# Row maximum of two of sixteen attention steps taken in two passes, one for each PSUM bank of scores

## What is computed

```
att = jnp.einsum('bqhd,bkhd->bhqk', q, k) * scale
att = jnp.where(causal, att, -jnp.inf)
att = jax.nn.softmax(att, axis=-1)
y = jnp.einsum('bhqk,bkhd->bqhd', att, v)
```

## Time and profile before

| | us |
|---|---|
| median of 3 runs | 3212.84 (3212.77 to 3213.65) |
| the profiled execution's own time | 3214.32 |
| its span | 3212.5 |
| PE busy | 3121.6 (97% of the span) |
| DVE busy | 2058.3 (64%) |
| ACT busy | 1946.8 (61%) |
| POOL busy | 1547.1 (48%) |
| granted TensorE clock | 0.993 of full |

### The profile page before, as it was taken

The page is one execution under the profiler, slowest core; times in us unless marked ns, Lnnn a source line. Parts: engine busy times, 40 slices in busy tenths (PEclk is TensorE's granted clock), DMA queues, the critical chain, the costliest instruction groups (busy, mean ns, idle before and its releaser), DMA issues. The chain is left out here.

```text
span 3212.5 us, 62152 instructions
## 1 busy us (share of the span) xinstructions
PE 3121.6 (97%) x20524; PEld 2515.9 (78%) x20524; DVE 2058.3 (64%) x5922; ACT 1946.8 (61%) x4189; POOL 1547.1 (48%) x1623
## 2 busy tenths in 40 slices
PE   8999999999999999999999999989989999999996
PEld 6777776777777677777777777769989999999996
DVE  5676666666667666666666666663878874445445
ACT  6676676666667666676766667655544444444444
POOL 3343343434434343343434434336766776666655
PEclk9999999999999999999999999999989999999998
DMA  5444454444445444444444444447744444433425
GB/s 135 103 116 97 102 126 102 107 115 94 109 102 125 102 105 112 97 112 115 108 103 106 109 115 112 99 139 267 282 156 96 105 118 103 106 88 88 107 49 155
DMA packets 213234, 376.61 MB, mean 117 GB/s; under 512 B 26280, under 2 KB 136232, under 8 KB 212928
## 3 DMA queue, kind: packets, MB, share of 16 engines
q1 hardware_dynamic: 170880, 322.20, 38.5%
q0 software_dynamic: 25152, 33.75, 6.2%
q10 hardware_dynamic: 16896, 16.78, 1.5%
HBM read 129.28 MB, written 75.59 MB: 64 GB/s over the span
## 5 line engine op out<-in xcount | busy, mean ns | idle before, releaser
L232 POOL TENSOR_SCALAR prob<-prob,inv 128x128 f32<-128x128 f32 (+7 forms) x1024 | 775.6, 757 | 1283.5 <-DVE inv L665 1276.7
L660 DVE CUSTOM_DVE_ANT_0 s_ps<-s_ps,mask 128x128 f32<-128x128 f32 (+7 forms) x1024 | 781.5, 763 | 659.9 <-PE s_ps L373 643.6
L550 ACT ACTIVATE prob<-s_ps,neg_max 128x128 f32<-128x128 f32 (+7 forms) x1024 | 759.6, 742 | 340.9 <-DVE neg_max L660 325.7
L388 PE MATMUL t_ps<-ident,prob 128*128 128x128 f32 x4096 | 611.3, 274 | 1.0 <-ACT prob_t L643 0.5
L643 ACT ACTIVATE prob_t<-t_ps 128x512 f32<-128x512 f32 (+3 forms) x704 | 376.8, 535 | 280.7 <-PE t_ps L388 274.0
L404 PE MATMUL o_ps<-prob_t,v 128*64 128x512 f32 (+3 forms) x3072 | 537.5, 492 | 1.5 <-DVE c_res L683 1.5
L388 PEld LDWEIGHTS t_ps<-ident,prob 128*128 128x128 f32 x4096 | 474.8, 140 | 52.6 <-issue 2.8
L404 PEld LDWEIGHTS o_ps<-prob_t,v 128*64 128x64 f32 x3072 | 204.1, 136 | 286.1 <-issue 267.2
L732 DVE COPY prob_t<-t_ps 128x128 f32<-128x128 f32 (+3 forms) x704 | 321.4, 456 | 27.6 <-PE t_ps L388 27.5
L1678 PE MATMUL e_y<-w_hi,hid_hi 128*128 128x256 f32 (+1 forms) x1088 | 312.2, 287 | 0.0
L1680 PE MATMUL e_y<-w_hi,hid_lo 128*128 128x256 f32 (+1 forms) x1088 | 308.2, 283 | 0.0
(11 more groups left out here) (259 smaller groups left out, 6226.0 us busy)
## 6 DMA issues: line engine op xcount, KB each, us to landing
k_hh<-k_high SPq DMA_DIRECT2D x128, 256.0 KB, 4.2
y_d<-c_res SPq DMA_DIRECT2D x128, 256.0 KB, 3.9
k_lz<-k_low SPq DMA_DIRECT2D x126, 256.0 KB, 5.1
w_lo<-k_high SPq DMA_DIRECT2D x124, 256.0 KB, 4.1
c_yt<-y_d SPq DMA_DIRECT2D x60, 512.0 KB, 6.9
q_hl<-q_high SPq DMA_DIRECT2D x64, 256.0 KB, 3.5
q_hl<-q_low SPq DMA_DIRECT2D x64, 256.0 KB, 4.3
b_xt<-w SPq DMA_DIRECT2D x16, 1024.0 KB
```

The source lines that it names most:

```text
L232: pool.tensor_scalar(pr, pr, inv[:, s % 4:s % 4 + 1], 1.0, ALU.mult, ALU.mult).then_inc(norm_done, 1)
L388: mm = pe.transpose(turned_in(s, k)[:, j * P:(j + 1) * P], prob[s % 4][:, (first + j) * P:(first + j + 1) * P], ident[:])
L550: act.activation(prob[s % 4][:, 0:(q + 1) * P], s_ps[s % 2][:, 0:(q + 1) * P], ACT.Exp, scale=-1.0, bias=neg_max[:, s % 4:s % 4 + 1], accu ...
L660: dve.tensor_tensor_reduce(part, part, mask[:, T - (q + 1) * P:T], 1.0, -MASKED, ALU.add, ALU.min, neg_max[:, s % 4:s % 4 + 1]).then_inc(m ...
```

## The change

In steps 13 and 15 of each pair TensorE signals `scores_done` after each of the two banks, 18 signals a pair where there were 16. VectorE's `maximum` runs two instructions there: a `tensor_reduce` with the minimum over the first bank's 512 columns, which the mask does not touch, into `neg_first`, and then the old instruction over the second bank's columns alone (384 in step 13, 512 in step 15), with `neg_first` as its beginning. Before the second there is a wait for the first one's own signal on `max_done`, a wait for the second bank, and a `sem_inc`. `max_done` too has 18 signals a pair. `scored(n, s)` gives the count at which step s is whole, and `exp` and the one wait of SyncE go by it. Nothing else moves.

```diff
+        neg_first = sb("neg_first", [P, 1])
...
+        BY_BANK = (13, 15)
+
+        def scored(n, s):
+
+            n, s = n + s // 16, s % 16
+            return (16 + len(BY_BANK)) * n + s + 1 + sum(t <= s for t in BY_BANK)
...
-                    sp.wait_ge(scores_done, 16 * (NPAIRS - 1))
+                    sp.wait_ge(scores_done, scored(NPAIRS - 2, 15))
...
-                mm.then_inc(scores_done, 1)
+                    if c == g or s in BY_BANK:
+                        mm.then_inc(scores_done, 1)
...
-                act.wait_ge(max_done, 16 * n + s + 1)
+                act.wait_ge(max_done, scored(n, s))
...
-                dve.wait_ge(scores_done, 16 * n + s + 1)
+                least, width, first = neg_max[:, s % 4:s % 4 + 1], (q + 1) * P, -MASKED
+                begin = 0
+                if s % 16 in BY_BANK:
+
+                    dve.wait_ge(scores_done, scored(n, s) - 1)
+                    dve.sem_inc(passed, 1)
+                    begin, first = HALF, neg_first[:, 0:1]
+                    dve.tensor_reduce(first, s_ps[s % 2][:, 0:HALF], AX.X, ALU.min).then_inc(max_done, 1)
+                    dve.wait_ge(max_done, scored(n, s) - 1)
+                dve.wait_ge(scores_done, scored(n, s))
                 dve.sem_inc(passed, 1)
 
-                part = s_ps[s % 2][:, 0:(q + 1) * P]
-                dve.tensor_tensor_reduce(part, part, mask[:, T - (q + 1) * P:T], 1.0, -MASKED, ALU.add, ALU.min,
-                                         neg_max[:, s % 4:s % 4 + 1]).then_inc(max_done, 1)
+                part = s_ps[s % 2][:, begin:width]
+                dve.tensor_tensor_reduce(part, part, mask[:, T - width + begin:T], 1.0, first, ALU.add, ALU.min,
+                                         least).then_inc(max_done, 1)
```

## The result

Over 20 runs of each, the changed kernel takes 3219.09 us (3217.79 to 3219.99) and the kernel before 3213.51 us. The ratio is 1.0018, with an interval of 1.0012 to 1.0024: 5.6 us slower, clear of no change, and just inside the 0.2% that I had set as what one comparison can tell. The range held the time (3204 to 3220), but it came out at its upper end, next to the 3219.0 of rival B, and 6 us above the forecast's own 3213.1. One execution of the kernel before took 4831.66 us, counts as slow and is left out of the ratio.

The account below looks back on a forecast made before the run. TensorE bounds it, busy 97%, its weight loads waiting for ScalarE's exponentials. Gains of 1.7 us (step 13) and 0.3 (pair 62 and drain) less 2.3 (m = 6) make 0.3 us slower: median 3213.1 us, range 3204 to 3220.

Parts of the forecast that it names:

- rival B: The reduction is longer than a copy, or its start value costs time: 3219.0 us, 3249 at the bound; chance 0.09.
- slack in ordinary pairs: The next pair's step 1 load does not wait for step 15's exponential; its slack rises from 0.07 to 0.21 us.
- The head start of 0.35 us: In step 13 the first bank's last matmul ends 0.35 us before the second's, with VectorE idle then.
- rival C: The first bank's signal comes no sooner than the last, so no head start: 20.5 us slower, 3233; chance 0.02.
- rival B's near case: A reduction of 0.755 us or a start value costing 0.09: step 13 loses 0.06 us, 6.2 us slower, 3219.0.
- gap: Between the reduction's end and the second pass: 0.19 us, for a wait on the reduction's signal and a `sem_inc`.
- step 13, first bank to `neg_max`, against unsplit: 1.48 us with the split against 1.51 without: 0.03 us gained in each of 57 pairs, 1.7 us.
- step 15 where m = 6: VectorE comes late from the latents, so no head start: 0.33 us lost in each of seven pairs, 2.3 us.
- A beginning read from a [128, 1] tile: Start value of the second pass, taken as free; bounded from above by 0.09 us for a separate load.
- the sign of 0.72 us: Where m = 6, the next pair's step 1 load would stand idle 0.72 us in place of 0.39.
- Rival A: The gap between reduction and second pass is 0.03 us, not 0.19: 10.2 us faster, 3202.6 us; chance 0.15.
- The cover by ScalarE: Step 13's gain cannot exceed 0.22 us, as ScalarE is busy with a copy and waited just that long for `neg_max`.

Follow-up runs that it names:

- step 15 alone: The changed kernel with the split in step 15 and not in step 13: 3216.13 us, ratio 1.0006 to the kernel before.

## Why the prediction was right, and where its sizes were off

What bounds the kernel was read right. The load of step 15 waits for the exponential of step 13 in 57 pairs, and that of step 1 for the exponential of step 15 in the seven with m = 6; no other step moved in every pair. That step 15 has slack in ordinary pairs held: with step 15 alone they kept their length, and in the changed kernel the load of step 1 starts 0.19 us after the exponential ends, where one that waits starts after 0.05. The head start of 0.35 us was there; rival C falls.

The range held, but not by the forecast's sum: that said a loss of 0.3 us, as good as no change, and the loss was 5.6, clear of no change. It lies 0.9 us inside the range's end, which had been set to take in rival B's near case. The sum was off since each term around the passes was a little off. Measured against predicted:

| term | predicted | measured |
|---|---|---|
| start of the first operation behind the signal | 0.19 | 0.15 |
| reduction, 512 columns | 0.67 | 0.69 |
| gap | 0.19 | 0.22 |
| second pass and readout, 384 columns | 0.62 | 0.68 |
| second pass and readout, 512 columns | 0.755 | 0.82 |
| step 13, first bank to `neg_max`, against unsplit | -0.03 | +0.04 |
| step 15 where m = 6 | +0.33 | +0.44 |
| slack of the load of step 1, ordinary pairs | 0.21 | 0.14 |
| gain of that load in pair 62 | 0.14 | 0.07 |
| idle time of the load of step 1 where m = 6 | 0.72 | 0.46, and 0.39 ahead of the turns |

The term that was mis-sized most is "A beginning read from a [128, 1] tile instead of a constant I take as free": it costs 0.06 us in every second pass, 57 x 0.06 + 7 x 0.06 = 3.8 us of the 5.3 that are missing, and with the constant the loss fell from 5.6 to 1.2 us. The gap (0.03 more) and the reduction (0.02 more) add 64 x 0.05 = 3.2 us, and the start that came 0.04 sooner takes 57 x 0.04 = 2.3 back in step 13: 4.7 us together. The price of the start value was one of the two causes that rival B named, at up to 0.09 us, and B had a chance of 0.09; the measured time is nearly B's near case (3219.0), and this half of B is what happened, while its other half, a reduction of 0.755 us, did not. The forecast had put a cost with no row of its own at one end of its bounds, at zero, where the middle would have been as well founded.

One path was not drawn to its end: where m = 6 the copy queued behind the second pass holds up TensorE's turns too. It changed no time, since the load of step 1 still starts 0.05 us after the exponential, but it is why the sign of 0.72 us did not show.

Rival A's gap of 0.03 us is wrong for the kernel as written; only its remark that the reduction might start sooner was right in part (0.15 us and not 0.19). Its arithmetic holds for another kernel: with the `sem_inc` moved ahead of the wait, the gap did fall to 0.04 us and the kernel got faster, by 6 and not 10 us because of the longer second pass and what the pairs with m = 6 lose. The prediction charged "about 0.16 us to a `sem_inc`"; the runs say 0.11 us for the first ahead of a reduction (0.15 against 0.04 over the pairs), 0.15 ahead of a custom pass (0.19 against 0.04), 0.18 where it carries two waits (0.22 against 0.04), and 0.09 for a further one. And having found that price in the rows of before, the prediction did not ask what it costs in the other passes, where 33 us lay.

The cover by ScalarE was read too tight: idle time of 0.22 us in front of the exponential, but 0.34 us of room. The change did not come near either, so this decided nothing here.

## What to carry to other kernels

A pass split in two pays the fixed costs of an operation again: here 0.69 + 0.22 + 0.68 us for what took 1.16, against a head start of 0.35. Before splitting, look for instructions between the wait and the work, and take them out or pass them while the engine is busy; here TensorE's loads of steps 7, 10 and 15 each got 0.15 us back. A cost for which there is no row belongs in the sum at the middle of its bounds, not at zero. Where VectorE and not the signal is late, a split has no head start and only costs.

## What the runs showed of the hardware

- A semaphore increment that VectorE passes after a wait delays what follows by 0.11 us (ahead of a reduction) or 0.15 us (ahead of a custom pass) for the first and 0.09 us for the next one; passed while an operation runs, it costs nothing (second pass 0.09 us before the reduction's end). One that carries waits for two semaphores has a record of 49 or 50 ns where the others have 21, and the second pass behind it starts 0.03 us later.
- The wait for its own operation's signal costs VectorE 0.12 us: the next operation starts 0.04 us after the end instead of 0.08 before it. The Trainium skill, "VectorE: DVE Perf Modes", section "The DRAIN you can't avoid", has it that eight copies take the same time with a semaphore behind each as with one behind the last. No run here has such a chain; these runs show a cost where the second pass waits for the reduction just issued.
- A custom pass over PSUM whose start value is read from a tile is 0.06 us longer than from a constant: 626 against 567 ns over 384 columns in the same place, 759 against 694 over 512 beside the plain passes of before.
- With its operand ready, an exponential on ScalarE starts 0.12 us before the record of the copy ahead of it ends (994.36 against 994.48).
- A minimum over 512 columns of PSUM takes 0.69 us, as a copy of them does (0.68).
- Open: why a `sem_inc` costs 0.04 us more ahead of a custom pass than ahead of a reduction. The `sem_inc` itself starts 0.04 us after the scores in both, so the difference lies behind it; it was not tried apart.
